# Products that nobody reads, issued in TensorE's waits in the last third of each joint pass of a two-layer language model tower

## The reference

```python
h = tok_ref(x, wids, ...)            # gather word rows and word vectors, LN, a gate between the two
h = h + attn0(layernorm(h), ...)     # 12 heads of 16; cumulative sums over the tokens, written as
                                     # causal masked products of keys and queries
h = h + ffn0(layernorm(h), ...)      # scores by token; the 19 lowest tokens of a sequence go through
                                     # softmax attention, the others through a pooled mix; then a
                                     # 192 -> 768 -> 192 layer with gelu
h = h + attn1(layernorm(h), ...)     # 12-head softmax attention with folded low-rank weights
h = h + moe(layernorm(h), ...)       # 8 experts, the two best of each token, 192 -> 768 -> 192
```

## Time and profile before

| | us |
|---|---|
| median of three executions (877.9 to 880.11) | 879.14 |
| the profiled execution, its own time | 878.32 |
| its span, first to last instruction | 876.3 |
| TensorE busy (83% of the span) | 729.2 |
| VectorE busy (59%) | 520.1 |
| ScalarE busy (35%) | 303.9 |
| GpSimd busy (28%) | 243.4 |

### The profile page before, as it was taken

One profiled execution on the slowest core, in us unless ns is written; L12 is line 12 of the kernel. 1 busy time (PEld: TensorE's weight loads), 2 busy tenths in 40 slices (PEclk: granted clock), 3 DMA queues, 4 the chain that ended last, 5 costly groups with the idle time before them and its releaser, 6 DMA issues.

```text
span 876.3 us, 15714 instructions
## 1 busy us (share of the span) xinstructions
PE 729.2 (83%) x5548; PEld 561.7 (64%) x5549; DVE 520.1 (59%) x1766; ACT 303.9 (35%) x700; POOL 243.4 (28%) x302
## 2 busy tenths in 40 slices
PE   1888777989678998867899976868878989999993
PEld 0546465566457565656666555757756989998892
DVE  7558757873678785668877476891434553333330
ACT  0033232624333263433244344223323433333330
POOL 5332200460013246001443300142000453333332
PEclk9999989999978999998899997797956999999998
DMA  7960000000000000000122000019301233222220
GB/s 251 411 247 1 1 1 1 19 8 1 1 1 28 27 19 8 1 2 1 37 35 9 1 3 1 1 55 344 90 1 29 43 73 47 38 37 38 36 35 8
DMA packets 29894, 43.63 MB, mean 50 GB/s; under 512 B 5355, under 2 KB 24597, under 8 KB 29830
## 3 DMA queue, kind: packets, MB, share of 16 engines
q1 hardware_dynamic: 19250, 30.87, 10.2%
q0 software_dynamic: 8752, 9.07, 6.5%
q10 hardware_dynamic: 1828, 2.84, 0.9%
HBM read 21.36 MB, written 22.09 MB: 50 GB/s over the span
## 4 chain that ended last, share of the span: by engine, by line
PE 59%; DVE 21%; issue 5%; ACT 5%; DMA 4%; POOL 4%; ACTq 1%; SPq 1%; POOLq 0%; DVEq 0%
PE qa L1898 26%; PE qc L1898 24%; PE qa L1901 4%; PE qc L1901 4%; DMA out<-qk_T 3%; DVE mx L1487 2%; POOL arena_w L438 1%; DVE st L1058 1%; ACT big L814 1%; DVE ctxT L1442 1%; DMA mu_row<-in_mu 1%; DVE qk_T L1493 1%; DVE arena_b L1425 1%; ACTq L641 1%; DVE arena_e L1299 1%
## 5 line engine op out<-in xcount | busy, mean ns | idle before, releaser
L1898 PE MATMUL qc<-arena_w,big 128*128 x468 | 82.8, 327 | 1.4 <-DVE qk_T L1877 1.4
L1898 PEld LDWEIGHTS qc<-arena_w,big 128*128 128x128 f32 x468 | 75.1, 190 | 2.1 <-issue 2.0
L1898 PE MATMUL qa<-arena_b 128*128 128x128 f32 (+2 forms) x688 | 73.1, 287 | 2.9 <-DVE att L1503 2.1
L1898 PEld LDWEIGHTS qa<-arena_b 128*128 128x128 f32 (+2 forms) x688 | 64.5, 191 | 11.5 <-DVE att L1503 2.5
L1898 PE MATMUL qa<-arena_e,nT 128*128 128x192 f32 (+2 forms) x256 | 69.9, 429 | 1.1 <-DVE ga L1369 0.7
L1024 ACT ACTIVATE big<-qa,arena_b 128x128 f32<-128x128 f32 x156 | 43.1, 375 | 74.9 <-PE qc L1898 68.4
L611 POOL DMA_INDIRECT out<-qk_T x39 | 61.0, 1565 | 20.6 <-issue 11.1
L1866 DVE COPY arena_b<-qc 128x256 f32<-128x256 f32 x39 | 16.6, 426 | 81.3 <-PE qc L1901 81.3
L1898 PEld LDWEIGHTS qa<-arena_e,nT 128*128 128x128 f32 x256 | 47.2, 200 | 22.9 <-issue 12.9
L474 POOL TENSOR_TENSOR rs_a<-rs_a,minus_half 128x8 f32<-128x8 f32 x4 | 6.6, 1644 | 175.5 <-DVE rs_a L1336 175.5
L1898 PE MATMUL qc<-qk_T 32*128 32x128 f32 (+1 forms) x680 | 33.5, 321 | 17.9 <-DVE qk_T L1493 13.5
(11 more groups left out here) (390 smaller groups left out, 1598.5 us busy)
## 6 DMA issues: line engine op xcount, KB each, us to landing
slots<-xk SPq DMA_DIRECT2D x1, 13192.0 KB, 41.8
arena_e<-in_w SPq DMA_DIRECT2D x8, 579.0 KB, 8.1
arena_w<-in_w SPq DMA_DIRECT2D x8, 576.0 KB, 9.4
qk_T<-slots SPq DMA_DIRECT2D x39, 97.0 KB, 1.9
out<-hb SPq DMA_DIRECT2D x16, 96.0 KB, 1.7
arena_e<-in_w_l SPq DMA_DIRECT2D x1, 804.0 KB
arena_e<-in_W ACTq DMA_DIRECT2D x1, 768.0 KB
out<-qk_T POOLq DMA_INDIRECT x39, 3.5
```

Of the source, the lines that this page charges most:

```text
L1898: return nc.tensor.matmul(o, l, r, start=start, stop=stop)
```

## The change

A function `hold(bank, n)` is added. It issues n products of 256 columns of `w_1q` (a weight that is not changed after set-up) against 32 columns of the identity. They wait for nothing, signal nothing, and what they write is overwritten by the next step that uses that bank. Eleven calls are put into `joint`, 24 products in all for each of the three passes. Nothing else changes on any engine.

```diff
+            def hold(bank, n):
+                for _ in range(n):
+                    mm(bank[0:32, 0:256], ident[:, 0:32], w_1q[:, 0, 0:8, :].rearrange("p h d -> p (h d)"))
...
                 o_T(tb, 1)
+                hold(QC[:, 3, :], 1)
                 logits(tb, 2)
                 av(ta, 3)
+                hold(QA[:, 2, :], 2)
                 max_T(tb, 2)
                 ob_T(ta, 3)
                 logits_T(tb, 2)
+                hold(QA[:, 2, :], 3)
                 av1(tb, 2)
+                hold(QC[:, 3, :], 1)
                 o_T(tb, 2)
...
                 max_T(tb, 3)
+                hold(QC[:, 3, :], 5)
                 logits_T(tb, 3)
+                hold(QA[:, 2, :], 1)
                 n3_T(ta, 0)
                 n3_T(ta, 1)
                 av1(tb, 3)
+                hold(QC[:, 3, :], 1)
                 o_T(tb, 3)
...
                 select(ta)
+                hold(QC[:, 3, :], 2)
                 queries(ta)
+                hold(QC[:, 3, :], 1)
                 counts(tb)
...
                 word_vectors(ta + 1)
+                hold(QC[:, 3, :], 5)
                 mix(ta, 0)
...
                 context(ta, 1)
+                hold(QC[:, 3, :], 2)
                 selected(ta, 0)
```

## The result

The changed kernel took 863.25 us (median of four runs, 862.97 to 864.99), the kernel before beside it 879.62 us (four runs, 877.9 to 880.21): ratio 0.9821, 95% interval 0.9802 to 0.9841.

The account below looks back on a forecast made before the run. The prediction took TensorE, 59% of the chain, with its clock often not whole, to bound the kernel. Savings of 4.2 (A), 2.6 (B) and 2.3 us (C), 9.1 in all, took 878.32 to 869.2 us; range 865.0 to 873.8.

Parts of the forecast that it names:

- C: Start of `values` to DVE's first product at line 1416, each joint pass: 2.3 us less in all, ends 0 and 4.6.
- A: Start of `logits(tb, 2)` to DVE's second add behind `wo`: 14.30 us at whole clock, 4.2 us less over three passes.
- B: DVE's second add behind `wo` to the start of `values`, each joint pass: 2.6 us less over three passes.
- D: Stretch behind C, first L1416 of a pass to its first L1449; the sum had no saving or loss there.
- Additions cost nothing at full clock: The 24 products a pass, 10.4 us, all lie in TensorE's waits if the clock is whole: cost nothing.
- The draining rival: A product without a reader still runs when the wait ends: 0.16 us at 33 places, 5.3 us back, 874.5 us; chance 6%.
- The clock follows short waits: Step: products filling short TensorE waits in the joint passes keep its clock up; narrow weights of 32 columns count.
- I let what is saved stand: Behind C, `mix` to the next pass: same pieces in all passes, no DMA wait, so nothing saved is lost.
- C is whole too: Rival: C at whole clock in all passes; 4.2 + 3.2 + 4.6 = 12.0 us less, 866.3 us; chance 15%.
- The clock rival: The clock does not follow short waits; products at half clock overrun by 3.1 us in all: 881.4 us, slower; chance 6%.
- the VectorE rival: VectorE and ScalarE take TensorE's place in A and B; only 4.5 us would be left: 873.8 us; chance 8%.
- no change: Case: the kernel changes by no more than 0.3%, parts of the others cancelling; chance 5%, given as 0.06 in the end.

Follow-up runs that it names:

- set 4: Later set on one chip; its "same kernel" is the changed kernel unaltered beside the kernel before: 864.35 us, ratio 0.9855.
- the kernel of set 4 with all products: Changed kernel plus products in the first pass, early joint passes and the back, with GpSimd's scatters behind `ln1_root`: 861.15 us, ratio 0.98 to the kernel before.
- set 3: Later set on one chip; the changed kernel run unaltered beside the kernel before: 883.06 us, ratio 1.0022.
- the last calls alone: Kernel before with only the last four calls (behind `select`, `queries`, `word_vectors`, `context`), 10 products a pass: 877.45 us, ratio 0.9981.
- products in the back too: Changed kernel with 28 more products in thirteen waits of the stretch behind the last joint pass: 856.36 us, ratio 0.9749; run again in set 3: 876.36 us, 0.9956.
- products everywhere: Changed kernel with 28 more products behind the last pass, 20 in the first pass, 4 early in each joint pass: 873.53 us (0.9857), again 869.09 us (0.9866).

## Why the prediction was right in its mechanism and wrong in its size

Two steps failed: the term for C (2.3 us forecast, 4.2 measured), and the nothing that the sum had for all outside the windows A, B and C (1.5 us ahead of A in the result's own runs, and later the lengthening of D).

- **Additions cost nothing at full clock.** Shown. The waits shrank by the added time and the released steps did not move (A 14.30 and B 13.97 us in all passes). The draining rival did not show: no step behind a filled wait is later. Twice the products cost 0.6 us in A and 1.3 in B, so the waits hold little more than was put in.
- **The clock follows short waits.** Shown, from both sides: it is whole in A and B with 256 columns a product, and falls as before with 8. Nor is it luck of the execution: in the 14 profiled kernels with single counts or one product a wait ahead of and in A, it took 14.30 to 14.31 us in all 42 passes; in the five with none there, or with 8 columns, in 3 of 15. The Trainium skill, page "TensorE: Matmul & The Clock Gate", section "Why this matters for your kernels", asks for no idle gaps of more than about 3 us; the traces disagree for the joint pass: in the kernel before the clock fell there though no wait was longer than 2.92 us, at 239.85 with none above 1.63 us ahead, and filling waits of 0.65 to 2.92 us was worth what is above. They don't contradict it in D, where the clock fell in waits of 3.09 and 3.27 us.
- **A, 4.2 us, and B, 2.6 us.** Measured 4.24 and 2.7.
- **C, 2.3 us.** This is the term of the sum that was mis-sized. I took half of 4.6, since "nothing is added among the short products of `gate` and `select`". Measured 4.2. The length at whole clock, 15.2 us, was right (15.11), and so was the doubt: in two of three passes the clock still falls there. What I had wrong is how long a fall lasts and what it costs. C at 0.89 is 15.3 and 15.6 us, only 0.2 to 0.5 above whole; the earlier trace rows had it at 0.70 and 0.79, 16.5 and more, and I had given a partly held clock the whole of that; the falls that were left lasted 3.4 us, where those of before lasted 6.8 to 10.2. Nor is it settled that C does so well each time: in set 4 the same kernel had C of pass 3 at 16.64 us. When the fall is a long one the price is worse than before: in the kernel of set 4 with all products C took 18.2 us in two passes, at 0.72. It had 10.2 us at half clock there, as C of pass 2 had before the change, where it took 16.99 us (16.97 with products of 8 columns; 17.81 with two products in C in place of three). So the products run at half clock too, and are paid for.
- **Outside the windows.** The sum had nothing there, neither for the part of a pass ahead of A nor for front, back and tail. The measured 12.8 us in the passes (4.2 + 2.7 + 4.2, 1.5 ahead of A and 0.1 in D) are 3.7 more than forecast and would by themselves have given 878.3 - 12.8 = 865.5 us, within the range. The rest to the profiled 865.0 is back -4.7, front +2.8 and tail +1.5, of which the unchanged kernel's own executions show as much (back 84.2 and 78.0 us). The median of the four, 863.25, is 1.7 us below the profiled run, and that step below the range has no place in any trace: it is within what executions of one kernel differ by.
- **"I let what is saved stand" behind C.** That held in the result's own runs. In three later sets it didn't: the copy behind `probs_T` is released late there while GpSimd scatters, and in the one of them in which the changed kernel was run unaltered (set 3) it was no faster than the kernel before. I had looked at what TensorE waits for behind C, and not at what had moved nearer to it: the scatters end 1.3 us later against the transposes than before (8.88 and 7.57 us behind L1416).
- **The rivals.** "C is whole too" was nearest (4.2 of its 4.6 in C). The clock rival and the VectorE rival did not show; no change is what set 3 measured, for a reason that none of my rivals named. The lower end of the range, one more short half-clock stretch gone, came nearest to the 1.5 us ahead of A.

## What to carry to other kernels

Where the same stretch takes two lengths in two passes at two granted clocks, the shorter one is what a held clock gives, and products without a reader in the waits ahead of the fall give it (256 columns here; 8 did nothing). They cost nothing while they fit the wait at full clock; seven more where the wait was 0.25 us cost 1.8 us a pass. Fill all such stretches at once: with the last calls alone nothing was left of their gain. Then ask what the shortened stretch has moved towards what comes next: here eight scatters, with which on some occasions the reports of finished matmuls come late; in the set where that was tried, the changed kernel unaltered was no faster than the kernel before. Of the versions run, the one with products in the back too was best on one chip (0.9749), that with products everywhere in the two sets with late reports in which it ran (0.9857 and 0.9866); those with the scatters later in passes 1 and 2 only, and products in the back, were not tried.

## What was not expected of the hardware

- While GpSimd issues a row of indirect scatters (eight, 1.3 us apart), semaphore updates of matmuls that are done may be seen 3 us late, with the copy that waits for them 1.4 to 1.9 us behind the end of the last scatter (8.88 and 10.49; 8.87 and 10.67 us behind L1416), in three of seven sets of runs; in the others, by the same program, the updates come 0.01 to 0.02 us behind the matmuls.
- One product of 256 columns against 32 columns of weights in each of eleven waits kept the clock of A whole (14.30 us, three passes); twenty-four of 8 columns did not (16.12 us in two of three passes).
- The same code behind the last pass took 84.2, 79.5, 78.0 and 82.2 us in four executions, at clocks of 0.72, 0.83, 0.88 and 0.75, and 73.6 us in all five profiled ones in which its waits were filled and the scatters were not moved.
